# First batch in another order, FFN weight transposes spread over the tail, gate half of the in-projection in the third batch

## The chip, the cores and the metric

The kernel runs on one core of a Trainium2 chip. The metric is the device time of one execution in microseconds (us). The core has a matrix engine (PE, whose weight loads are listed as PEld), a vector engine (DVE), a scalar engine (ACT), GpSimd (POOL), and a queue engine (SP) that issues most DMAs. Every engine works through its own list of instructions in order, and the lists are tied together by semaphores alone.

## The reference

One layer over 64 sequences of 32 rows (D = 512), each with 257 context rows:

```python
x = x + cross_attention(layernorm(x), ctx, mask)        # 16 heads of 32
x = x + mamba(layernorm(x))
x = x + ffn_int8(layernorm(x))                          # 512 -> 2048 -> 512, quantised

# mamba: d_inner 1024, 16 states, 4 taps
x_, z = split(x @ in_proj_w)                            # z: the gate half
x_ = silu(conv4(x_) + conv_b)
B, C, d = split(x_ @ x_proj_w)
dt = softplus(d * dt_w + dt_b)
h_t = exp(dt*A) * h_(t-1) + dt*x_*B_t ;  y_t = sum_n h_t*C_t
y = (y + x_*D) * silu(z);  return y @ out_proj_w
# ffn: weights are quantised per row; the activations by their global maximum
```

## The kernel before

The 2048 rows are 16 tiles of 128 rows, and one tile is four sequences (batches b = 0 to 3). `schedule` is called once for each engine with a class that holds that engine's part of every step, so the text of `schedule` is the program order of every engine. It runs 17 stages: `interval(ta, tm, to, more)` does the attention of tile `ta`, the first part of the mamba of `tm = ta - 1` ("front"), and its end for `to = ta - 2` ("back"). Interval 0 has attention only (with the quantisation of the FFN weights), interval 1 has attention and front, intervals 2 to 14 have all three, interval 15 has all three but no next tile, and `tail` finishes the mamba of the last two tiles and starts the FFN phase.

Inside an interval each batch b does the following. PE computes `scores` (L987) for this batch, transposes the next batch's context (`kv_transpose`, L921), computes its keys (`kv_keys`, L955) and its values in two halves (`kv_values`, L966), transposes the probabilities (`transpose_p`, L996) and weighs the values (`weigh_values`, L1005). ACT copies each of these out of PSUM and takes the exponentials (`softmax`, L1245; `normalise`, L1282). DVE makes one pass over the scores of each head group (L1623) and the reciprocal of the sums (L1636).

The mamba work lies between these steps. The scan of a tile is 32 DVE steps in the order of `CHAIN`: for each of 8 channel chunks c a product (c,0) (L1736), a scan (c,1) (L1741, 4.4 us), a product (c,2) (L1747, 2.3 us) and a sum (c,3) (L1713, L1718). ACT makes the factors, `decays` (c, half), in 16 groups of eight exponentials (L1390). `place(name)` calls put them at named places of a batch, by the tables `FINISH`, `BEGIN`, `FINISH_DECAYS` and `BEGIN_DECAYS`.

In batch 0 of an interval stand `x1_write` (DVE, L1650; it waits for PE's `wo_product` of the interval before, L1020), `mamba_norm`, `mamba_turn` (PE, L1051), `mamba_in` (the x half of the in-projection, 64 matmuls, L1058), the taps on ACT (L1326), `mamba_conv` (DVE, L1677), the SiLU (ACT, L1333) and `mamba_bcd` (PE, L1085). In batch 1 stand `dt_row`, `mamba_steps`, `mamba_softplus` (ACT), `mamba_dt` (DVE, L1691), `mamba_gate` (the gate half, 64 matmuls, L1058), `mamba_gated`, `mamba_out` (PE, L1099), `gate_silu` (ACT, two table loads around two SiLUs, L1355 to L1357) and `out_sum` (DVE, L1821). `scores` of batch 2 waits for `out_sum`. In batches 2 and 3 come the next tile's queries (`ln_q_rows`, `q_transpose` L1027/L1240, `q_product` L1039, `q_spread` L1275); `kv_transpose` in batch 3 waits for the copy xnT (L1240), because both use bank 0. Batch 3 ends with `wo_product`.

`kv_keys` in batch b = 2 waits for `gate_silu`, because keys and in-projection share banks 6 and 7; for the same reason each half of `mamba_gate` waits for one `keys_copy` (L1224).

Of the kernel before, what the change touches and what calls it, by code (L numbers as in the profile page):

```python
# [6 lines left out]
P = 128  # L7
# [32 lines left out]
def perceiver_kernel(nc, x, ctx_kv, mask, Wq, bq, Wk, bk, Wv, bv, Wo, bo, Win, conv_w, conv_b, Wx,  # L40
# [13 lines left out]
    with ExitStack() as ctx:  # L54
# [216 lines left out]
        tail_summed = sem("tail_summed")  # L271
        tail_kept = sem("tail_kept")
# [16 lines left out]
        wq_loaded = [sem("w1q_loaded"), sem("w2q_loaded")]  # L289
# [40 lines left out]
        FINISH = {(0, "a"): range(21, 22), (0, "b"): range(22, 25), (0, "c"): range(25, 28),  # L330
# [7 lines left out]
        FINISH_DECAYS = {(0, "n"): ((6, 1),), (0, "t"): ((7, 0), (7, 1))}  # L338
# [9 lines left out]
        def tail(part):  # L348
# [4 lines left out]
            part.decays(PREV, ((6, 1), (7, 0)))  # L353
# [6 lines left out]
            part.decays(PREV, ((7, 1),))  # L360
# [5 lines left out]
            part.weigh(PREV, 6)  # L366
            part.mamba_conv(LAST)
            part.gate(PREV, 5)
            part.mamba_silu(LAST)
            part.mamba_bcd(LAST, 0)  # L370
# [24 lines left out]
            for c in range(1, IC):  # L395
# [3 lines left out]
                for n in range(6 * (c - 2), min(2 * FC, 6 * (c - 1)), 3) if c > 1 else ():  # L399
                    part.weights_transpose(range(n, min(2 * FC, n + 3)))  # L400
                if c == 2:
                    part.out_sum(PREV)
                    part.out_norm(PREV)
                    part.out_rstd(PREV)
                    part.out_rows(PREV)
                    part.out_max(PREV)
                part.gate(LAST, c - 1)
                part.weigh(LAST, c)
                part.sum_states(LAST, c)
# [19 lines left out]
        def schedule(part, engine):  # L429
            part.load_context(0)  # L430
            part.load_x(0)
            part.kv_transpose(0, 0)
# [4 lines left out]
            part.kv_values(0, 0)  # L437
            part.values_copy(0, 0)
            part.kv_values(0, 1)
# [10 lines left out]
            def interval(ta, tm, to, more):  # L450

                here, front, back = ta is not None, tm is not None, to is not None
                for b in range(BT):
# [14 lines left out]
                    if b == 0 and front:  # L468
                        part.x1_write(tm)
                        part.mamba_norm(tm)  # L470
                    if b == 0 and here:
                        part.load_bias(ta)
                        part.residual(ta)
                    if here:
                        part.scores(g, ta, b, to)
                    if following:
# [9 lines left out]
                    if b == 2 and here and more:  # L486
                        part.ln_q_rstd(ta + 1)
                    if b == 3 and back:
                        part.out_rstd(to)
                    if b > 0:  # L490
                        place("a")
                    if here:
# [12 lines left out]
                    if following:  # L505
                        part.kv_keys(g + 1, b, ta, tm, to, more)
                    if b == 0 and front:
                        part.mamba_rows(tm)
                        part.mamba_turn(tm, keys)
                    if following and b == 0:  # L510
                        part.kv_values(g + 1, 0)
                    if following and b > 0:
                        part.keys_copy(g + 1, 0)
                    if here:
                        part.normalise(g)
                    if b == 0 and front:
                        part.mamba_transpose(tm, keys)
                    if following and b == 0:
                        part.keys_copy(g + 1, 0)
                    place("n")  # L520
                    if following:
                        part.keys_copy(g + 1, 1)
                    place("k")
# [14 lines left out]
                    if b == 0 and front:  # L538
                        part.mamba_taps(tm, 0)
                        part.mamba_pad(tm, 1)  # L540
# [8 lines left out]
                    if following and b > 0:  # L549
                        part.kv_values(g + 1, 0)  # L550
# [22 lines left out]
                    if b == 1 and front:  # L573
                        part.gate_silu(tm)
                    if following:
                        part.kv_values(g + 1, 1)
                        part.values_copy(g + 1, 1)
                    if b == 2 and here and more:
                        part.q_transpose(ta + 1)
                    place("d")  # L580
                    if b == 0 and front:
                        part.mamba_bcd(tm, keys)
# [19 lines left out]
        class Part:  # L602
# [3 lines left out]
            def weights_prepare(self, b, name): pass  # L606
            def weights_load(self): pass
            def weights_transpose(self, pieces): pass
            def kv_transpose(self, g, rows): pass
            def kv_keys(self, g, b, ta, tm, to, more): pass  # L610
            def keys_copy(self, g, j): pass
            def kv_values(self, g, h): pass
# [77 lines left out]
        def wT_out(n):  # L690
            if n < FC:
                return w1qT[:, :, n * P:(n + 1) * P]
            j, q = (n - FC) // 4, (n - FC) % 4
# [30 lines left out]
        def _(sp):  # L724
# [3 lines left out]
            class Loads(Part):  # L728
# [87 lines left out]

                def weights_load(self):
# [3 lines left out]
                    for i in range(4):  # L821
                        sp.wait_ge(wq_stored[i], 16)
                    sp.dma_start(w1q, w1q_dram.rearrange("(i p) d -> p i d", p=P)).then_inc(wq_loaded[0], 16)
                    sp.dma_start(w2q, w2q_dram.rearrange("(j p) f -> p j f", p=P)).then_inc(wq_loaded[1], 16)
# [68 lines left out]
        def _(pe):  # L893
# [10 lines left out]
            class Products(Part):  # L904
# [4 lines left out]
                def kv_transpose(self, g, rows):  # L909

                    pe.wait_ge(ctx_loaded, 16 * (g + 1))
                    for i in range(2):
                        if i == 0:
                            wait(pe, v_copied, 2 * g - 1 if not isinstance(g, int) or g else 0)
                            wait(pe, xnT_copied, 1 if isinstance(g, int) and g == 1 else rows)
                        else:
                            wait(pe, v_copied, 2 * g)
                        for c in (2 * i, 2 * i + 1):
                            for h in range(2):
                                at = (c % 2) * KF + h * P  # L920
                                last = pe.transpose(bank[i][:, at:at + P], ctx_sb[:, h, c * P:(c + 1) * P], idf[:])  # L921
                        last.then_inc(ctxT_psum, 1)
# [9 lines left out]
                def kv_keys(self, g, b, ta, tm, to, more):  # L932
# [5 lines left out]
                    for j in range(2):  # L938
# [8 lines left out]
                        if b == 2 and tm is not None:  # L947
# [12 lines left out]
                def kv_values(self, g, h):  # L960
# [4 lines left out]
                    for c in range(DC):  # L965
                        last = pe.matmul(bank[h][:], ctxT[:, c, h * P:(h + 1) * P], wv_sb[:, c, :],  # L966
                                         start=(c == 0), stop=(c == DC - 1))
                    last.then_inc(v_psum, 1)
# [133 lines left out]
                def weights_transpose(self, pieces):  # L1102
                    for n in pieces:
# [7 lines left out]
                        for k in range(4):  # L1111
                            src = (w1q[:, n, k * P:(k + 1) * P] if n < FC
                                   else w2q[:, (n - FC) // 4, (4 * ((n - FC) % 4) + k) * P:(4 * ((n - FC) % 4) + k + 1) * P])
# [3 lines left out]
                def sum_states(self, t, c):  # L1117
                    i = item(t, c)

                    wait(pe, tail_gated, i - 1)  # L1120
                    for n in range(NS):
                        if n % (NS // 2) == 0:
                            pe.wait_ge(tail_weighed, 2 * i + 1 + n // (NS // 2))
                        pe.matmul(bank[i % 2][:, 0:P], idf[:], state(i)[:, n, :], start=(n == 0), stop=False)  # L1124
# [829 lines left out]
```

## Time and profile before

| what | us |
|---|---|
| median of 3 runs (2095.92 to 2097.03) | 2096.26 |
| the profiled execution's own time | 2097.7 |
| its span, first to last instruction | 2095.9 |
| an interval of the loop, from one end of `wo_product` to the next | 113.9 |
| busy in the interval 1033.96 to 1147.86: DVE / PE / ACT | 107.7 / 106.8 / 98.3 |
| from the end of interval 15 (1830.2) to the first FFN matmul (1971.8) | 141.6 |

Interval 1 lasts 107.8 us, interval 2 112.8 us, interval 15 113.4 us. PE's mean granted clock over the span is 0.971 of full speed. Busy time alone does not say which engine sets an interval: each engine waits a little at a few places, and what counts is which of those waits lies on the loop of releases that closes from one interval to the next.

### The profile page before, as it was taken

To read this page: it belongs to the slowest core of one execution; us is meant where nothing else is said; L and a number is where in the kernel's file an instruction comes from. 1 tells how busy PE (TensorE), PEld (TensorE's weight loads), DVE (VectorE), ACT (ScalarE), POOL (GpSimd) and SP (SyncE) were. 2 spreads that over 40 slices of the span, in tenths; PEclk is the share of its full clock that TensorE was granted. 3 is DMA by queue.
4 is the path that set the end of the run, shared out by engine and by line. 5 is a ranking of instruction groups with operands and counts; after the bars stand their busy time and mean duration, and the time that the engine had idled before them with its cause. 6 is when DMAs were issued, how large, how long until landed. Compare 5 with 4: busy or idle time off the path is not lost. (4 is left out here: it accounts for less than half of the span.)

```text
span 2095.9 us, 37583 instructions
## 1 busy us (share of the span) xinstructions
PE 1921.6 (92%) x11655; PEld 1360.5 (65%) x11670; DVE 1853.5 (88%) x2313; ACT 1675.9 (80%) x4617; POOL 475.2 (23%) x397
## 2 busy tenths in 40 slices
PE   7998999999999999999999999999999999667799
PEld 5676766667676666676666767666666667466444
DVE  1546999999999999999999899999999999998688
ACT  3358989888979889888889897988988888867484
POOL 1001213031413122131304131312213131300013
PEclk9999999999999999999999999999999999888899
DMA  9522333233342332333324334233333332230214
GB/s 280 211 81 86 76 92 82 83 83 88 72 110 65 75 99 61 101 81 88 76 80 87 94 70 98 71 76 94 71 101 81 88 75 77 61 122 11 71 40 141
DMA packets 93396, 188.55 MB, mean 90 GB/s; under 512 B 18768, under 2 KB 39904, under 8 KB 88160
## 3 DMA queue, kind: packets, MB, share of 16 engines
q1 hardware_dynamic: 78448, 133.32, 19.6%
q0 software_dynamic: 14832, 54.01, 13.9%
q8 instruction: 33, 0.54, 0.1%
q14 instruction: 83, 0.68, 0.1%
HBM read 116.12 MB, written 17.18 MB: 64 GB/s over the span
## 5 line engine op out<-in xcount | busy, mean ns | idle before, releaser
L1390 ACT ACTIVATE dA<-dt,A_sb 128x124 f32<-128x124 f32 x2048 | 616.1, 394 | 14.4 <-DVE dt L1691 10.2
L1741 DVE TENSOR_TENSOR_SCAN hb<-dA,hb 128x2048 f32<-128x2048 f32 x118 | 522.4, 4427 | 8.1 <-ACT dA L1390 4.3
L955 PE MATMUL bank<-ctxT,wk_sb 128*128 128x256 f32 x2048 | 463.7, 384 | 21.6 <-ACT ctxT L1208 15.3
L966 PE MATMUL bank<-wv_sb,ctxT 128*128 128x512 f32 x1024 | 463.2, 595 | 2.3 <-ACT ctxT L1208 2.3
L955 PEld LDWEIGHTS bank<-ctxT,wk_sb 128*128 128x128 f32 x2048 | 384.9, 191 | 86.4 <-ACT ctxT L1208 19.2
L1484 POOL DMA_DIRECT2D hb<-hb x103 | 93.3, 906 | 1023.6 <-DVE hb L1747 1009.1
L966 PEld LDWEIGHTS bank<-wv_sb,ctxT 128*128 128x128 f32 x1024 | 186.8, 191 | 195.9 <-issue 195.8
L1736 DVE TENSOR_TENSOR hb<-u,BC 128x2048 f32<-128x2048 f32 x118 | 270.4, 2291 | 5.7 <-DVE u L1703 2.6
L1747 DVE TENSOR_TENSOR hb<-hb,BC 128x2048 f32<-128x2048 f32 x117 | 268.0, 2290 | 1.1
L1058 PE MATMUL bank<-xn2T,win_sb 128*128 128x128 f32 x2048 | 236.4, 277 | 0.7 <-ACT xn2T L1307 0.7
L1058 PEld LDWEIGHTS bank<-xn2T,win_sb 128*128 128x128 f32 x2048 | 234.8, 194 | 1.9 <-ACT xn2T L1307 1.1
L1459 POOL TENSOR_SCALAR maskn<-maskb 128x257 f32<-128x257 f32 x64 | 146.5, 2290 | 182.8 <-DVE soft L1623 155.0
L1245 ACT ACTIVATE Pr<-Pr,soft 128x257 f32<-128x257 f32 x256 | 127.4, 507 | 62.2 <-DVE soft L1623 61.9
L1713 DVE TENSOR_TENSOR hb<-hb 128x512 f32<-128x512 f32 (+2 forms) x248 | 149.4, 602 | 4.5
L1677 DVE SCALAR_TENSOR_TENSOR xs<-xpad,convw,xs 128x128 f32<-128x128 f32 x384 | 106.8, 346 | 51.1 <-ACT xs L1326 49.4
L1208 ACT ACTIVATE ctxT<-bank,lastT 128x256 f32<-128x256 f32 x256 | 100.8, 476 | 58.7 <-PE bank L921 58.7
L1005 PEld LDWEIGHTS bank<-PT,V 128*128 128x128 f32 x1024 | 123.5, 194 | 28.6 <-issue 28.6
L1282 ACT ACTIVATE Pr<-Pr,soft 128x256 f32<-128x256 f32 x256 | 108.9, 503 | 27.5 <-DVE soft L1636 27.5
L1005 PE MATMUL bank<-PT,V 128*128 128x128 f32 x1024 | 127.6, 278 | 2.8 <-ACT PT L1299 2.8
L1224 ACT ACTIVATE KT<-bank,bqkv 128x256 f32<-128x256 f32 x256 | 106.0, 467 | 28.5 <-PE bank L955 28.5
L1231 ACT COPY V<-bank 128x512 f32<-128x512 f32 x128 | 74.8, 584 | 63.5 <-PE bank L1005 41.8
L1445 POOL TENSOR_SCALAR stats<-stats 128x1 f32<-128x1 f32 x48 | 53.2, 1108 | 289.2 <-DVE stats L1539 289.2
(158 smaller groups left out, 2606.8 us busy)
## 6 DMA issues: line engine op xcount, KB each, us to landing
hb<-hb POOLq DMA_DIRECT2D x103, 512.0 KB, 4.8
ctx_sb<-in_ctx_dram SPq DMA_DIRECT2D x64, 512.0 KB, 3.9
BC<-bcd_dram SPq DMA_DIRECT2D x32, 1024.0 KB, 7.1
maskb<-in_mask_Bx1x1xS_fk_dram SPq DMA_DIRECT2D x64, 128.5 KB, 3.3
wstage<-in_L_ffn_w_dram SPq DMA_DIRECT2D x4, 2048.0 KB, 11.9
x_sb<-in_x_dram SPq DMA_DIRECT2D x16, 256.0 KB, 3.5
win_sb<-in_L_attn_in_proj_w_dram SPq DMA_DIRECT2D x1, 4096.0 KB, 24.4
bo_sb<-bias_dram SPq DMA_DIRECT2D x64, 64.0 KB, 2.0
```

Of the source, the lines that this page charges most:

```text
L955: last = pe.matmul(bank[6 + j][:, (m % 2) * KF:(m % 2 + 1) * KF], wk_sb[:, c, m * P:(m + 1) * P], ctxT[:, c, :], start=(c == 0), stop=(c = ...
L966: last = pe.matmul(bank[h][:], ctxT[:, c, h * P:(h + 1) * P], wv_sb[:, c, :], start=(c == 0), stop=(c == DC - 1))
L1005: last = pe.matmul(bank[4][:, m * P:(m + 1) * P], V[:, h, m * P:(m + 1) * P], PT[:, h, m, :], start=(h == 0), stop=(h == 1))
L1058: last = pe.matmul(bank[6 + q % 2][:, e * P:(e + 1) * P], win_sb[:, c, n:n + P], xn2T[:, c, :], start=(c == 0), stop=(c == DC - 1))
L1245: act.activation(Pr[:, m, :], Pr[:, m, :], ACT.Exp, scale=-1.0, bias=soft[:, 0, m:m + 1], accum_out=soft[:, 1, m:m + 1]).then_inc(exp_done, 1)
L1282: act.mul(Pr[:, m, 0:KF], Pr[:, m, 0:KF], soft[:, 2, m:m + 1]).then_inc(p_ready, 1)
L1390: last = act.activation(dA[:, c % 2, n * BT:(n + 1) * BT, 1:], dt[:, c, :].rearrange("p (b s) -> p b s", s=S)[:, :, 1:], ACT.Exp, scale=A_ ...
L1459: pool.tensor_scalar(maskn[:], maskb[:], -NEG, 1.0, ALU.mult, ALU.mult).then_inc(mask_scaled, 1)
L1713: dve.tensor_tensor(tile[:, 0:n, :], tile[:, 0:n, :], tile[:, n:2 * n, :], ALU.add).then_inc(sum_step, 1)
L1736: ins = dve.tensor_tensor(tile, u[:, c, :].unsqueeze(1).broadcast_to([P, NS, P]), BC[:, 0:NS, :], ALU.mult)
L1741: ins = dve.tensor_tensor_scan(flat, dA[:, c % 2].rearrange("p n s -> p (n s)"), flat, 0.0, ALU.mult, ALU.add)
L1747: ins = dve.tensor_tensor(tile, tile, BC[:, NS:2 * NS, :], ALU.mult)
```

## The change

In batch 0 of an interval: `mamba_norm` follows `scores`; decays (6,1) stand ahead of the exponentials (a new place "s"), (7,0) at "n", (7,1) between the two halves of the taps ("h"); the first half of `kv_values(.., 0)` is ahead of `mamba_turn` and the second half after `mamba_in`; scan step 25 goes ahead of the convolution; `mamba_bcd` goes from the end of batch 0 to batch 1 behind `scores`; the table load behind the SiLU comes after the second values copy. `kv_transpose` on PE becomes `kv_turn` in two halves, and in batches 1 and 2 the first stands ahead of `scores`. `mamba_gate` goes from batch 1 to batch 2 (ahead of `transpose_p`), and `gate_silu` from batch 1 to batch 2 (ahead of the second values copy). In the tail the FFN weight transposes are spread (5, 3, then 4 for each chunk from the third on, w2 first, loaded earlier), `out_max` moves back behind `weigh`, and the last chunk's states are partly summed on DVE.

```diff
-        FINISH = {(0, "a"): range(21, 22), (0, "b"): range(22, 25), (0, "c"): range(25, 28),
+        FINISH = {(0, "a"): range(21, 22), (0, "b"): range(22, 26), (0, "c"): range(26, 28),
...
-        FINISH_DECAYS = {(0, "n"): ((6, 1),), (0, "t"): ((7, 0), (7, 1))}
+        FINISH_DECAYS = {(0, "s"): ((6, 1),), (0, "n"): ((7, 0),), (0, "h"): ((7, 1),)}
...
-                        part.mamba_norm(tm)
...
+                    if following and 0 < b < BT - 1:
+                        part.kv_turn(g + 1, 0, 0)
                     if here:
                         part.scores(g, ta, b, to)
+                    if b == 0 and front:
+                        part.mamba_norm(tm)
+                    if b == 1 and front:
+                        part.mamba_bcd(tm, keys - DC)
+                    if following and 0 < b < BT - 1:
+                        part.kv_turn(g + 1, 0, 1)
...
+                    if following and b == 0:
+                        part.kv_values(g + 1, 0, range(0, 2))
...
                     if b == 0 and front:
                         part.mamba_in(tm, keys)
+                    if following and b == 0:
+                        part.kv_values(g + 1, 0, range(2, DC))
...
                     if b == 1 and front:
                         part.mamba_softplus(tm)
+                        part.mamba_dt(tm)
+                    if b == 2 and front:
                         part.mamba_gate(tm, keys)
-                        part.mamba_dt(tm)
                     place("b")
...
-                    if b == 1 and front:
+                    if b == 2 and front:
                         part.gate_silu(tm)
                     if following:
-                        part.kv_values(g + 1, 1)
+                        part.kv_values(g + 1, 1, range(DC))
                         part.values_copy(g + 1, 1)
+                    if b == 0 and front:
+                        part.mamba_table(tm)
...
-                        if b == 2 and tm is not None:
+                        if b == 3 and tm is not None:
                             pe.wait_ge(zs_ready, 2 * tm + j + 1)
...
-                for n in range(6 * (c - 2), min(2 * FC, 6 * (c - 1)), 3) if c > 1 else ():
-                    part.weights_transpose(range(n, min(2 * FC, n + 3)))
+                if c > 1:
+                    part.weights_transpose(range(4 * c, 4 * (c + 1)))
...
+                    if t == LAST and c == IC - 1:
+                        dve.wait_ge(tail_weighed, 2 * i + 2)
+                        for k, n in enumerate((4, 2)):
+                            wait(dve, tail_folded, k)
+                            dve.tensor_tensor(state(i)[:, 8:8 + n, :], state(i)[:, 8:8 + n, :],
+                                              state(i)[:, 8 + n:8 + 2 * n, :], ALU.add).then_inc(tail_folded, 1)
```

## Rows read from the trace of the kernel before

**Rows 1.** Busy time by engine in two intervals; PEclk is the granted clock.

```profile
1033.96:1147.86 113.90, 106.77 (x673) 76.40 (x681) 107.70 (x135) 98.26 (x282) 30.87 (x24) 1.00 0.34 82
1261.21:1375.11 113.90, 108.26 (x673) 77.13 (x680) 107.73 (x134) 98.13 (x282) 29.48 (x24) 0.99 0.35 83
```

**Rows 2.** The same for batches 0, 1 and batches 2, 3 of one interval.

```profile
1033.96:1099.53 65.57, 61.02 (x390) 45.02 (x390) 60.07 (x89) 53.51 (x142) 7.37 (x10) 1.00 0.30 82
1099.53:1147.86 48.33, 45.75 (x283) 31.38 (x291) 47.63 (x47) 44.74 (x141) 23.50 (x15) 1.00 0.40 83
```

**Rows 3.** Timeline of DVE, that interval: start, us, instruction, idle before it.

```profile
1038.66 0.67 DVE L1650 TENSOR_TENSOR x<-bank,xbo 128x512 f32<-128x512 f32 x1
...
1043.34 0.18 DVE L1636 RECIPROCAL soft<-soft 128x4 f32<-128x4 f32 x1 [1.11 <-ACT Pr L1245]
...
1056.47 6.76 DVE L1677 SCALAR_TENSOR_TENSOR xs<-xpad,convw,xs 128x128 f32<-128x128 f32 x24 [2.44 <-ACT xs L1326]
...
1098.65 0.68 DVE L1821 CUSTOM_DVE_ANT_0 x<-bank,x 128x512 f32<-128x512 f32 x1
```

**Rows 4.** Timeline of PE, that interval.

```profile
1036.97 7.17 PE L955 MATMUL bank<-ctxT,wk_sb 128*128 128x256 f32 x32 [1.03 <-ACT ctxT L1208]
...
1064.45 1.93 PE L1085 MATMUL bank<-xs,wx_sb 128*33 128x128 f32 x16 [2.89 <-ACT xs L1333]
...
1075.41 7.31 PE L1058 MATMUL bank<-xn2T,win_sb 128*128 128x128 f32 x64
1082.55 1.04 PE L996 MATMUL bank<-idf,Pr 128*128 128x128 f32 x8
...
1086.86 1.95 PE L1005 MATMUL bank<-PT,V 128*128 128x128 f32 x16
...
1099.60 0.73 PE L987 MATMUL bank<-KT,Q 32*32 32x257 f32 x32 [0.49 <-DVE stats L1821]
...
1121.87 1.06 PE L921 MATMUL bank<-idf,ctx_sb 128*128 128x128 f32 x8 [0.79 <-ACT xnT L1240]
...
1130.73 3.72 PE L955 MATMUL bank<-ctxT,wk_sb 128*128 128x256 f32 x16 [0.77 <-ACT Q L1275]
```

**Rows 5.** Timeline of ACT, that interval.

```profile
1036.44 1.57 ACT L1208 ACTIVATE ctxT<-bank,lastT 128x256 f32<-128x256 f32 x4 [0.72 <-PE bank L921]
1041.23 0.51 ACT L1245 ACTIVATE Pr<-Pr,soft 128x257 f32<-128x257 f32 x1 [3.22 <-DVE soft L1623]
...
1082.30 2.42 ACT L1390 ACTIVATE dA<-dt,A_sb 128x124 f32<-128x124 f32 x8 [0.65 <-DVE dt L1691]
1084.62 0.56 ACT L1297 COPY PT<-bank 128x512 f32<-128x512 f32 x1
...
1095.78 1.28 ACT L1355 ACT_TABLE_LOAD   x1 [0.59 <-PE bank L1099]
...
1098.17 1.28 ACT L1357 ACT_TABLE_LOAD   x1
...
1112.63 0.82 ACT L1224 ACTIVATE KT<-bank,bqkv 128x256 f32<-128x256 f32 x2
...
1116.62 0.58 ACT L1231 COPY V<-bank 128x512 f32<-128x512 f32 x1
...
1121.13 0.59 ACT L1240 COPY xnT<-bank 128x512 f32<-128x512 f32 x1
```

**Rows 6.** Timeline of PE in the tail: equal groups of 32 matmuls.

```profile
1882.69 5.46 PE L1124 MATMUL bank<-hb,idf 128*128 128x128 f32 x32 [5.75 <-DVE hb L1785]
...
1904.92 6.25 PE L1124 MATMUL bank<-hb,idf 128*128 128x128 f32 x32 [3.48 <-DVE hb L1785]
...
1936.89 3.81 PE L1124 MATMUL bank<-hb,idf 128*128 128x128 f32 x32
```

**Rows 7.** Timeline of DVE in the tail.

```profile
1903.26 0.16 DVE L1830 TENSOR_TENSOR xmax<-xmax 128x1 f32<-128x1 f32 x1 [2.18 <-POOL xmax L1501]
...
1962.10 0.29 DVE L1801 TENSOR_TENSOR win_sb<-bank,win_sb 128x128 f32<-128x128 f32 x1 [6.00 <-PE bank L1126]
```

More of the change, by code:

```diff
@@ L352, in tail @@
             part.kept_sum(PREV)
-            part.decays(PREV, ((6, 1), (7, 0)))
+            part.decays(PREV, ((6, 1),))
+            part.weights_transpose(range(0, 5))
             part.mamba_rows(LAST)
@@ L359, in tail @@
             part.sum_states(PREV, 5)
[L360 removed]
+            part.decays(PREV, ((7, 0),))
             part.feed(PREV, 6)
@@ L366, in tail @@
             part.weigh(PREV, 6)
+            part.decays(PREV, ((7, 1),))
+            part.weights_transpose(range(5, 8))
             part.mamba_conv(LAST)
@@ L431, in schedule @@
             part.load_x(0)
+            part.kv_turn(0, 0, 0)
+            part.kv_turn(0, 0, 1)
             part.kv_transpose(0, 0)
@@ L436, in schedule @@
             part.group_keys()
-            part.kv_values(0, 0)
+            part.kv_values(0, 0, range(DC))
             part.values_copy(0, 0)
-            part.kv_values(0, 1)
+            part.kv_values(0, 1, range(DC))
             part.values_copy(0, 1)
@@ L487, in interval @@
                         part.ln_q_rstd(ta + 1)
+                    if b == 3 and here and not more:
+                        part.weights_first()
                     if b == 3 and back:
@@ L506, in interval @@
                         part.kv_keys(g + 1, b, ta, tm, to, more)
+                    if following:
+                        part.keys_copy(g + 1, 0)
+                    if following and b == 0:
+                        part.kv_values(g + 1, 0, range(0, 2))
+                    if here:
+                        part.normalise(g)
+                    if b > 0:
+                        place("n")
                     if b == 0 and front:
                         part.mamba_rows(tm)
[L509 to L520, printed above, removed]
                     if following:
                         part.keys_copy(g + 1, 1)
+                    if b == 0 and front:
+                        part.mamba_turn(tm, keys)
+                        part.mamba_transpose(tm, keys)
+                    if b == 0:
+                        place("n")
                     place("k")
@@ L539, in interval @@
                         part.mamba_taps(tm, 0)
+                    place("h")
+                    if b == 0 and front:
                         part.mamba_pad(tm, 1)
@@ L549, in interval @@
                     if following and b > 0:
-                        part.kv_values(g + 1, 0)
+                        part.kv_values(g + 1, 0, range(DC))
                     if following:
@@ L907, in top_spread, with kv_turn @@
                     spread(bank[0][:, 0:P], xmax[:, 0:1]).then_inc(top_psum, 1)
[L909 to L922, printed above, removed]
+                def kv_turn(self, g, rows, i):
+                    if i == 0:
+                        pe.wait_ge(ctx_loaded, 16 * (g + 1))
+                        wait(pe, v_copied, 2 * g - 1 if not isinstance(g, int) or g else 0)
+                        wait(pe, xnT_copied, 1 if isinstance(g, int) and g == 1 else rows)
+                    else:
+                        wait(pe, v_copied, 2 * g)
+                    for c in (2 * i, 2 * i + 1):
+                        for h in range(2):
+                            at = (c % 2) * KF + h * P
+                            last = pe.transpose(bank[i][:, at:at + P], ctx_sb[:, h, c * P:(c + 1) * P], idf[:])
+                    last.then_inc(ctxT_psum, 1)
                 def last_values(self):
```

65 lines of the change are left out of this document (44 added, 21 removed).

## The prediction

> **What bounds the kernel now.** I read the page's shares first, then the windows of single intervals, then the timelines of DVE, PE and ACT through one of them. The thirteen full intervals (2 to 14) are 1480 of the 2096 us, so they decide. In one, DVE is busy for 107.70 us of 113.90, PE for 106.77, ACT for 98.26 [rows 1]. In another PE is busy 1.5 us longer, at a mean granted clock of 0.99, and the interval lasts 113.90 us all the same [rows 1]: PE has slack and DVE sets the length. The reader is to see that DVE's idle time is mostly two waits: 1.11 us for the exponentials and 2.44 us for the taps of the convolution, both in batch 0 [rows 3]. PE's longest wait, 2.89 us for the SiLU ahead of `mamba_bcd` [rows 4], costs nothing now. The second thing to see is how full the halves are: in batches 2 and 3 (48.33 us) PE is busy 45.75, DVE 47.63, ACT 44.74; in batches 0 and 1 (65.57 us) it is 61.02, 60.07 and 53.51 [rows 2]. The change gives room in the half that has some and puts work into the half that has none.
>
> Times below count from the end of `wo_product` at 1033.96.
>
> **What it takes away.** Decays (6,1) go into ACT's idle 3.22 us ahead of the exponentials [rows 5]. ACT then runs through: context copies from 2.5 to 4.05, decays (8 take 2.3 net of overlap), exponentials 2.1, so the reciprocal starts at 8.4 instead of 9.4 [rows 3, 5]; `mamba_norm` now lies in DVE's wait of 1.11. Between the reciprocal (9.38) and its wait for the taps (22.51 less 2.44) DVE has 10.7 us of steps [rows 3], and now step 25 too, 2.3. The taps come ahead of that: with the half of `kv_values` behind it the in-projection starts 1.7 earlier, and only one group of decays stands before the first taps instead of three. So the convolution runs from 21.4 to 28.1 without its wait of 2.44; it ended at 29.3 with step 25 still to do [rows 3]. DVE is then 3.3 us ahead, and the first decays of tile `tm` (48.34 before [rows 5]) start at 45.0. `mamba_bcd` waits for less: `kv_turn` and `scores` (1.2) fill the front of its 2.89 and the table load behind the SiLU no longer holds back the values copy. If nothing else followed, 3.3 us an interval would be won.
>
> **What it moves.** The gate half is 64 matmuls, 7.14 from start to start [rows 4], and two SiLUs between two table loads, from 1095.78 to 1099.45, 3.67 [rows 5]. Both leave batch 1.
>
> In batch 1 they were cover. ACT copies the transposed probabilities only behind decays (0,0), at 50.66 [rows 5]; PE spent the time on the gate half and weighed the values at 52.9 [rows 4]. Now these copies come at 47.3 to 48.4, while PE has ended keys, transposes and values by about 44.5: a new wait of 4. That wait costs little by itself, because `scores` of batch 2 waits for `out_sum` on DVE anyway (its wait of 0.49 [rows 4]). It comes at 65.64 less 3.3, 62.3. PE gets there with 7.14 us owed.
>
> In batch 2 they meet a full ACT. I keep the old numbers here and take off the 3.3 at the end. The first half of the in-projection waits for the first `keys_copy` (0.8), the second for the second, which ACT ends at 79.5 (1112.63 and 0.82 [rows 5]; DVE's reciprocal and two groups of decays stand before it, none of them moved). So PE ends the gate half at 79.5 + 3.6 = 83.1. Transposes and values take 4.3 (1082.55 to 1086.86), weighing 1.95: 89.4 [rows 4]. Behind it ACT has, in order, a values copy, the oT copies, decays (3,1), then `gate_silu`, the other values copy and xnT. Without `gate_silu` that is 5.1 (1116.62 to 1121.72); with it 8.8 [rows 5], so xnT is there at 98.2. PE, with values (3.4), `q_transpose` (0.5) and `scores` (0.7) behind the weighing, is ready at 94.0 and waits 4.3 for xnT, where it waited 0.79. `kv_transpose` starts at 98.3 instead of 87.91 [rows 4]. From there to the end of `wo_product` it is 26.0 as before (1121.87 to 1147.86), less the 0.77 for the queries, whose copies no longer are late: 25.2 [rows 4].
>
> **The sum for an interval:** 45.0 (to the first decays) + 50.0 (98.3 less 48.34) + 25.2 = 120.2. The next interval's ACT work hangs on the same end (oT copies, 16 decays, values copy), so the loop closes through PE, ACT and DVE in turn, and DVE, then with 12 us idle, does not bound it. Against 113.9 that is +6.3.
>
> **PE's clock comes on top.** After a wait of 3.48 us 32 matmuls took 6.25 instead of 3.81, after 5.75 us 5.46: 1.65 to 2.4 lost to the granted clock at its lower level of the two, 1.2 instead of 2.4 GHz [rows 6]. The 2.89 us wait sometimes brings it as well, that is the interval with 108.26 busy [rows 1]. The wait of 4.3 in batch 3 lies on the loop; I take 1.7 for it, the lower row, because PE is denser here; bounds 0 and 2.4. The same loss in batch 1 is covered. So 121.9, +8.0 an interval, x 13 = +104.
>
> The Trainium skill's "ScalarE: Activation LUTs", section "What ACT_TABLE_LOAD costs", puts a switch of tables at 1.28 us for the load and about 1.38 us to drain, which would make `gate_silu` 6.4 and the interval nearly 125. The trace has no such drain: load, SiLUs and load fill 3.67 us end to end [rows 5], and I stay with that.
>
> **The rest.** Interval 1 gets the same new wait for xnT without DVE behind it: +5 (0 to +7). Interval 15 has no xnT; only `gate_silu` delays its batch 3, less the head start: +1.5 (-3 to +3). In the tail, DVE's wait of 2.18 for `out_max` goes; the last sum of 32 matmuls, behind which DVE waits 6.00 [rows 7], becomes 20 and two small additions, -2.7; fewer weight copies per chunk -1: together -6 (-10 to 0). The earlier load of w2 waits for keys of batch 2 that are done when SP comes to it. Setup and interval 0 do the same work in nearly the same order: 0. Sum +0.5.
>
> The profiled execution took 2097.7 (span 2095.9 and 1.8 around it), 1.4 above the median of the runs. 2097.7 + 104 + 0.5 - 1.4 = **2201 us**.
>
> **Rivals.** (a) *Faster: DVE stays the bound.* DVE loses its two waits, PE fits the gate half into batches 2 and 3, and ACT clears batch 2 in time. The interval is then DVE's 113.9 - 3.3 = 110.6, the total 2096 - 43 - 6 = 2047. For it speaks that DVE is the busiest engine [rows 1] and that DVE and PE alone would need only about 110: DVE from `x1_write` to `out_sum`, 57, and PE from there 52 to 53. It is what the Trainium skill's "Perfetto Trace Analysis", section "Identifying the Most-Contended Engine", would have one expect: improve the engine with the highest occupancy first. Against it: xnT would have to be ready 4.3 us earlier and the second `keys_copy` 1 us earlier, and nothing before them on ACT is moved. It decides from there: if xnT comes before `scores` of batch 3, this is the result. 11 in 100. (b) *The chain holds only in part,* for instance because ACT is ahead at the start of an interval or the clock stays up: 114.4 to 119 us an interval, 2103 to 2163. 13 in 100. (c) *The clock falls at both new waits and stays down longer,* or the decays of chunk 2 slip too: above 124, over 2228. 8 in 100. (d) *It cancels:* 113.7 to 114.1. 2 in 100. My forecast, 119 to 124 an interval, is 2163 to 2228: 66 in 100.
>
> **Chances and range.** Within 0.2% is about what a measurement of this kernel can tell from no change. Slower is forecast, (b) and (c): 0.87; same 0.02; faster 0.11. The range of 8 in 10 leaves out (a), (d), the upper part of (c) and the very lowest of (b): 2120 to 2232. The likeliest case has 2163 to 2228 by itself.
>
> **What would show it.** Intervals near 120 to 122 us. On DVE the two waits of batch 0 gone, and new waits in batch 3 (for PE's scores and for decays). On PE about 4 us idle ahead of `weigh_values` in batch 1, about 1 us inside the gate half in batch 2, about 4 us ahead of `kv_turn` in batch 3, ended by xnT, with the granted clock down behind it. `out_max` without a wait in the tail. The prediction is wrong if that last wait is under 1 us, or if the first decays of the tile don't start near 45.

## The result: 5.4% slower, and the profile after

| | before | after |
|---|---|---|
| median, us (lowest to highest) | 2096.65 (2095.92 to 2098.36), 4 runs | 2208.88 (2208.24 to 2210.72), 4 runs |
| span of the profiled execution, us | 2095.9 | 2208.9 |
| intervals 2 to 14 together, us | 1478.93 | 1588.70 |

The ratio of the medians is 1.0536, 95% interval 1.0517 to 1.0554. The forecast was 2201 (2120 to 2232).

The windows over intervals 2 to 14, first of before, then of after (busy time of PE, PEld, DVE, ACT and POOL; PEclk is the third number from the end):

```profile
237.88:1716.81 1478.93, 1399.06 (x8618) 999.80 (x8624) 1399.32 (x1729) 1275.90 (x3654) 384.98 (x312) 0.99 0.34 83
```

```profile
242.89:1831.59 1588.70, 1433.75 (x8618) 1040.76 (x8624) 1402.05 (x1730) 1284.53 (x3653) 371.43 (x312) 0.96 0.31 78
```

The matmuls are the same in number, DVE's busy time grew by 2.7 us, ACT's by 8.6. PE's grew by 34.7 at the same work, since its granted clock fell from 0.99 to 0.96. The rest of the 109.8 us, 75.1, is PE waiting. An interval is 122.21 on average, against 113.76.

The timeline of PE in the interval from 1098.61 to 1220.71 of after (start, us, instruction, idle before it and what ended it). Its lines have moved: `kv_turn` is L955, `weigh_values` L1040, the in-projection L1093, `q_product` L1074, `wo_product` L1055.

```profile
1111.92 0.63 PE L1086 MATMUL bank<-idf,ln_out 128*128 128x128 f32 x4 [1.90 <-ACT ln_out L1292]
...
1146.86 3.52 PE L1040 MATMUL bank<-PT,V 128*128 128x128 f32 x16 [3.70 <-ACT PT L1341]
...
1169.93 3.84 PE L1093 MATMUL bank<-xn2T,win_sb 128*128 128x128 f32 x32 [0.61 <-ACT KT L1266]
1174.57 3.84 PE L1093 MATMUL bank<-xn2T,win_sb 128*128 128x128 f32 x32 [0.79 <-ACT KT L1266]
...
1188.30 0.72 PE L1022 MATMUL bank<-KT,Q 32*32 32x257 f32 x32
1193.48 1.94 PE L955 MATMUL bank<-idf,ctx_sb 128*128 128x128 f32 x8 [4.46 <-ACT xnT L1282]
1195.21 4.96 PE L1074 MATMUL bank<-xnT,wq_sb 128*128 128x128 f32 x32
...
1217.01 3.70 PE L1055 MATMUL bank<-wo_sb,oT 128*128 128x512 f32 x8
```

The reader is to see one long wait in each half: 3.70 us for the transposed probabilities in batch 1, and 4.46 us for xnT in batch 3, where [rows 4] have 0.79. ACT in the same interval:

```profile
1143.34 2.42 ACT L1434 ACTIVATE dA<-dt,A_sb 128x124 f32<-128x124 f32 x8 [0.34 <-DVE dt L1735]
1145.66 0.56 ACT L1339 COPY PT<-bank 128x512 f32<-128x512 f32 x1
...
1173.68 0.83 ACT L1266 ACTIVATE KT<-bank,bqkv 128x256 f32<-128x256 f32 x2
...
1185.02 1.09 ACT L1333 COPY oT<-bank 32x128 f32<-32x128 f32 x4
1186.13 2.42 ACT L1434 ACTIVATE dA<-dt,A_sb 128x124 f32<-128x124 f32 x8
1188.57 1.28 ACT L1399 ACT_TABLE_LOAD   x1
1189.87 1.08 ACT L1399 ACTIVATE zs<-bank 128x512 f32<-128x512 f32 x2
1190.97 1.28 ACT L1401 ACT_TABLE_LOAD   x1
...
1192.74 0.59 ACT L1282 COPY xnT<-bank 128x512 f32<-128x512 f32 x1
```

From 1185.02 to xnT ACT runs without a pause: oT copies, eight decays, `gate_silu` with its two table loads, a values copy, xnT. PE was ready at 1189.0. And DVE, which has lost its wait for the taps (L1721, the row of [rows 3] with 2.44) but gained three waits in batch 3:

```profile
1106.45 0.18 DVE L1680 RECIPROCAL soft<-soft 128x4 f32<-128x4 f32 x1 [1.34 <-ACT Pr L1287]
...
1119.83 6.65 DVE L1721 SCALAR_TENSOR_TENSOR xs<-xpad,convw,xs 128x128 f32<-128x128 f32 x24
...
1189.31 0.43 DVE L1667 CUSTOM_DVE_ANT_0 Pr<-bank,maskn 128x257 f32<-128x257 f32 x1 [3.36 <-PE bank L1022]
...
1198.39 0.18 DVE L1680 RECIPROCAL soft<-soft 128x4 f32<-128x4 f32 x1 [3.18 <-ACT Pr L1287]
...
1208.57 4.42 DVE L1785 TENSOR_TENSOR_SCAN hb<-dA,hb 128x2048 f32<-128x2048 f32 x1 [4.07 <-ACT dA L1434]
```

The granted clock behind the two long waits, by windows of the same trace (PEclk is again the third number from the end):

```profile
1146.86:1150.27 3.41, 3.41 (x17) 3.41 (x18) 3.17 (x4) 2.17 (x8) 0.00 (x0) 0.54 0.00 0
1191.24:1198.06 6.82, 4.58 (x23) 4.61 (x24) 3.98 (x1) 5.42 (x14) 4.18 (x1) 0.52 0.16 55
```

It is the lower level, 1.2 GHz, for 3.4 us behind the first wait and for 6.8 us around the end of the second. In intervals 2 to 14 before had 8 such stretches, 27 us in all; after has 25, 123 us. Behind the first wait the stretch is 3.4 us long in 10 of the 13 intervals, at the second it is 6.8 us long in 10.

### The profile page after: what moved, and what is told of

The parts are those of the page before. It is cut to its first block, busy times and chain, and to the rows that moved or that the text cites. A ratio compares the mean times of both kernels' runs of the same rounds, so it can differ in the third digit from the quotient of the medians.

```text
span 2208.9 us, 37587 instructions
## 1 busy us (share of the span) xinstructions
PE 1959.2 (89%) x11658; PEld 1403.2 (64%) x11658; DVE 1855.5 (84%) x2315; ACT 1685.8 (76%) x4617; POOL 461.3 (21%) x397
## 4 chain that ended last, share of the span: by engine, by line
PE 41%; ACT 21%; issue 10%; DVE 9%; POOL 2%; SPq 1%; DMA 1%; DVEq 0%; ACTq 0%; POOLq 0%
ACT dA L1434 9%; PE bank L1000 8%; PE bank L1093 7%; PE bank L1134 4%; PE bank L1040 4%; PE bank L989 3%; PE bank L1074 3%; PE bank L1197 3%; PE bank L1219 3%; PE bank L955 2%; ACT Pr L1324 2%; POOL stats L1489 1%; ACT KT L1266 1%; DVE hb L1791 1%; PE bank L1031 1%
## 5 line engine op out<-in xcount | busy, mean ns | idle before, releaser
L989 PE MATMUL bank<-ctxT,wk_sb 128*128 128x256 f32 x2048 | 456.6, 381 | 3.5 <-ACT ctxT L1250 3.4
L1093 PE MATMUL bank<-xn2T,win_sb 128*128 128x128 f32 x2048 | 244.6, 280 | 18.9 <-ACT KT L1266 18.2
L1093 PEld LDWEIGHTS bank<-xn2T,win_sb 128*128 128x128 f32 x2048 | 236.6, 195 | 29.8 <-ACT KT L1266 26.0
L1503 POOL TENSOR_SCALAR maskn<-maskb 128x257 f32<-128x257 f32 x64 | 154.5, 2413 | 318.6 <-DVE soft L1667 317.3
L1040 PEld LDWEIGHTS bank<-PT,V 128*128 128x128 f32 x1024 | 138.2, 212 | 92.8 <-issue 92.8
L1040 PE MATMUL bank<-PT,V 128*128 128x128 f32 x1024 | 142.0, 298 | 57.4 <-ACT PT L1341 57.4
L955 PE MATMUL bank<-idf,ctx_sb 128*128 128x128 f32 x512 | 91.9, 317 | 77.2 <-ACT xnT L1282 62.8
L1667 DVE CUSTOM_DVE_ANT_0 Pr<-bank,maskn 128x257 f32<-128x257 f32 x256 | 94.2, 422 | 65.9 <-PE bank L1022 65.6
L955 PEld LDWEIGHTS bank<-idf,ctx_sb 128*128 128x128 f32 x512 | 67.7, 161 | 121.7 <-ACT V L1273 76.4
```

What stands on the lines that cost most here:

```text
L989: last = pe.matmul(bank[6 + j][:, (m % 2) * KF:(m % 2 + 1) * KF], wk_sb[:, c, m * P:(m + 1) * P], ctxT[:, c, :], start=(c == 0), stop=(c = ...
L1040: last = pe.matmul(bank[4][:, m * P:(m + 1) * P], V[:, h, m * P:(m + 1) * P], PT[:, h, m, :], start=(h == 0), stop=(h == 1))
L1093: last = pe.matmul(bank[6 + q % 2][:, e * P:(e + 1) * P], win_sb[:, c, n:n + P], xn2T[:, c, :], start=(c == 0), stop=(c == DC - 1))
L1503: pool.tensor_scalar(maskn[:], maskb[:], -NEG, 1.0, ALU.mult, ALU.mult).then_inc(mask_scaled, 1)
```

## The experiments

Lines with a minus are those of the kernel named first. Intervals given are means over 2 to 14.

**gate_back.** The changed kernel with the gate half and its SiLU back in batch 1; everything else of the change kept.

```diff
                     if b == 1 and front:
                         part.mamba_softplus(tm)
+                        part.mamba_gate(tm, keys)
                         part.mamba_dt(tm)
-                    if b == 2 and front:
-                        part.mamba_gate(tm, keys)
...
-                    if b == 2 and front:
+                    if b == 1 and front:
                         part.gate_silu(tm)
...
-                        if b == 3 and tm is not None:
+                        if b == 2 and tm is not None:
                             pe.wait_ge(zs_ready, 2 * tm + j + 1)
```

> The changed kernel with the gate half and its SiLU back in the second batch, all else as changed. Theory (the ACT chain of batches 2 and 3 makes the loss, the rest of the change gains): an interval of 110.6 to 112 us, no wait for xnT over 1 us, total 2050 to 2070, faster than before. Rival (the new order of batch 0 or the moved x projection is part of the loss): over 2097.

Measured: 2042.79 us (2040.98 to 2043.9), ratio to before 0.9749 (0.9733 to 0.9766). One interval by windows, and PE's scores of batch 3 and its wait for xnT in it:

```profile
1117.94:1227.98 110.04, 106.70 (x672) 76.43 (x679) 107.38 (x133) 98.39 (x282) 30.54 (x24) 1.00 0.36 88
```

```profile
1201.19 0.72 PE L1021 MATMUL bank<-KT,Q 32*32 32x257 f32 x32
1202.69 1.06 PE L954 MATMUL bank<-idf,ctx_sb 128*128 128x128 f32 x8 [0.79 <-ACT xnT L1281]
```

An interval is 110.22 us on average. In the one shown DVE is busy for 107.38 of 110.04 us and waits 0.39 us at most; its longest wait in all 13 is 0.86. So the new order of batch 0 by itself is a gain of 3.5 us an interval, and the whole loss lies in the moved gate half. Here DVE does bound the loop, as rival (a) had it: what failed that rival was the move, not its account of the engines.

Side by side with the interval of the changed kernel above (122.10), this one shows where the 12.1 us of the move lie. `scores` of batch 3 start 89.7 us into the interval there and 83.3 here: 6.4 us, the moved half on PE with the two waits inside it, less 1.3 us that PE is ahead when batch 2 begins. From these scores to `kv_turn` it is 5.2 there and 1.5 here: 3.7 us, the longer wait for xnT. From `kv_turn` to the end it is 27.2 there and 25.3 here: 1.9 us, where the clock is down. So about half of the loss is PE's own displaced work; the late copy and what follows from it are the other half.

**gate_only.** The opposite: the kernel before, with only the gate half, its SiLU and the wait for it moved.

```diff
                     if b == 1 and front:
                         part.mamba_softplus(tm)
-                        part.mamba_gate(tm, keys)
                         part.mamba_dt(tm)
+                    if b == 2 and front:
+                        part.mamba_gate(tm, keys)
...
-                    if b == 1 and front:
+                    if b == 2 and front:
                         part.gate_silu(tm)
...
-                        if b == 2 and tm is not None:
+                        if b == 3 and tm is not None:
                             pe.wait_ge(zs_ready, 2 * tm + j + 1)
```

> The kernel before with the gate half and its SiLU alone moved to the third batch. Theory: the whole loss and a little more, since the 3.3 us of the new batch 0 are missing: an interval of 123 to 126 us, total 2225 to 2260. Rival (the loss needs the other edits, such as the split context transposes): under 2200.

Measured: 2251.74 us (2251.37 to 2252.11), ratio 1.075 (1.0728 to 1.0771). An interval is 125.12, 11.4 more than before; in the new order the same move costs 12.0 (110.22 to 122.21). The timeline of PE:

```profile
1169.38 3.12 PE L1006 MATMUL bank<-PT,V 128*128 128x128 f32 x16 [3.84 <-ACT PT L1300]
...
1216.01 1.94 PE L922 MATMUL bank<-idf,ctx_sb 128*128 128x128 f32 x8 [4.47 <-ACT xnT L1241]
```

The two long waits come with the move alone. The prediction's sum without its gain of 3.3 is 48.34 + 50.0 + 25.2 + 1.7 = 125.2: the two parts add up nearly as separate terms.

**pt_first.** Is the wait of batch 1 part of the loss? The changed kernel with decays (0,0) behind the copies of the probabilities.

```diff
-        BEGIN_DECAYS = {(1, "b"): ((0, 0),), (1, "p"): ((0, 1),), (1, "c"): ((1, 0),), (1, "w"): ((1, 1),),
+        BEGIN_DECAYS = {(1, "p"): ((0, 0), (0, 1)), (1, "c"): ((1, 0),), (1, "w"): ((1, 1),),
```

> The changed kernel with decays (0,0) behind the copies of the transposed probabilities in the second batch, so that PE's new wait of 3.7 us there shrinks to about 1.4. Theory (that wait is covered by DVE and out_sum): within 4 us of the changed kernel's 2208.9. Rival (it is on the loop): 2.3 us less in each of 13 intervals, about 2179.

Measured: 2212.88 us (2211.14 to 2214.62), ratio 1.0564 (1.0543 to 1.0585); an interval 122.6. PE's timeline:

```profile
1142.33 2.02 PE L1040 MATMUL bank<-PT,V 128*128 128x128 f32 x16 [0.94 <-ACT PT L1341]
...
1147.28 7.13 PE L1134 MATMUL bank<-wout_sb,zs 128*128 128x512 f32 x16 [2.93 <-DVE zs L1864]
```

The wait is now in two pieces, 0.94 and 2.93, the second for DVE ahead of `mamba_out`. The time is not better: in batch 1 PE waits because it is ahead of DVE, and the wait is covered, whatever name it bears.

**no_tables.** Is it ACT's time ahead of xnT? The changed kernel without the two table loads of `gate_silu`; its two activations are Identity in place of SiLU, so the gate is not computed.

```diff
                         act.activation(tile[:, 4 * i:4 * (i + 1), :].rearrange("p e q -> p (e q)"), bank[6 + i][:],
-                                       ACT.Silu).then_inc(zs_ready, 1)
-                    act.preload_act_table_set("natural_log_exp_and_others")
+                                       ACT.Identity).then_inc(zs_ready, 1)
```

> The changed kernel with plain copies in place of the two gate SiLUs and their two table loads (the gate is not computed): 2.57 us less on ACT in the third batch, the same work on PE. Theory (ACT's chain to xnT sets the interval, and the granted clock falls because of the wait): PE's wait for xnT falls from 4.47 to 1.9, the clock stays up there, an interval of 117 to 119 us, total 2140 to 2165. Rival 1 (ACT sets it, the clock costs nothing): 119.8, total 2175. Rival 2 (the matmuls moved are the loss): over 2200.

Measured: 2144.03 us (2142.66 to 2145.39), ratio 1.0236 (1.0215 to 1.0256). ACT, then PE:

```profile
1271.22 1.08 ACT L1399 ACTIVATE zs<-bank 128x512 f32<-128x512 f32 x2
1272.65 0.62 ACT L1282 COPY xnT<-bank 128x512 f32<-128x512 f32 x1
```

```profile
1273.42 1.06 PE L955 MATMUL bank<-idf,ctx_sb 128*128 128x128 f32 x8 [1.76 <-ACT xnT L1282]
```

2.56 us less on ACT (two loads of 1.28) takes 2.70 off PE's wait and 4.4 off the interval (117.80). By the averages over intervals 2 to 14, `kv_turn` starts 2.4 us earlier, and from there to the end it is 25.4 instead of 27.4. The second part is the clock's: 12 lower stretches with 58 us are left, against 25 with 123, and none of them lies behind xnT. An interval is still 7.6 us longer than in gate_back, with the matmuls still in batch 2: that part is not the table loads. No run moved the matmuls without the two activations.

**silu_late.** Is it the order on ACT? The changed kernel with `gate_silu` one step later in batch 2, behind `q_transpose`, so that xnT is copied first. Nothing is taken away.

```diff
-                    if b == 2 and front:
-                        part.gate_silu(tm)
                     if following:
                         part.kv_values(g + 1, 1, range(DC))
                         part.values_copy(g + 1, 1)
...
                     if b == 2 and here and more:
                         part.q_transpose(ta + 1)
+                    if b == 2 and front:
+                        part.gate_silu(tm)
```

> The changed kernel with the gate SiLU behind the xnT copy instead of ahead of the second values copy; no work added or left out. Theory (the place of these 3.67 us in ACT's order is what PE waits for): the wait for xnT falls under 1 us, a smaller one of 1 to 2 us comes ahead of the queries' product or the second half of the keys, the clock stays up, an interval of 118 to 120 us, total 2150 to 2180. Rival (ACT is simply full in batches 2 and 3, the order does not matter): within 5 us of 2209.

Measured: 2164.21 us (2160.94 to 2169.02), ratio 1.0322 (1.0299 to 1.0346); an interval 119.25. ACT, then PE:

```profile
1284.05 0.59 ACT L1282 COPY xnT<-bank 128x512 f32<-128x512 f32 x1
1284.65 1.28 ACT L1399 ACT_TABLE_LOAD   x1
```

```profile
1284.78 1.07 PE L955 MATMUL bank<-idf,ctx_sb 128*128 128x128 f32 x8 [0.78 <-ACT xnT L1282]
1287.09 3.84 PE L1074 MATMUL bank<-xnT,wq_sb 128*128 128x128 f32 x32 [1.24 <-ACT zs L1399]
...
1295.33 3.69 PE L989 MATMUL bank<-ctxT,wk_sb 128*128 128x256 f32 x16 [0.95 <-ACT Q L1317]
```

PE's wait for xnT is back at its old size, but `q_product` now waits for the SiLU, and the keys for the queries. The clock did not stay up, as the theory had it: in 8 of the 13 intervals it falls for 3.4 us around the start of `q_product`. Order alone is worth 3.0 us an interval, the clock's part in it included, a third of the 8.5 by which the changed kernel's interval is longer than before. Against gate_back 9.0 us are left: by the averages `kv_turn` still starts 6.5 us later (91.2 instead of 84.7), although its wait is the same, and that is PE's moved half; the other 2.5 come behind it.

**filler.** What does the granted clock take? The changed kernel with 16 products that nothing reads (32 matmuls in the trace), put on PE in front of the scores of batch 3, that is into its wait for xnT.

```diff
+                def filler(self):
+                    for k in range(16):
+                        pe.matmul(bank[5][:, 0:P], idf[:], wo_sb[:, 0, 0:P], start=True, stop=True)
...
+                    if b == BT - 1 and following and front and back:
+                        part.filler()
                     if here:
                         part.scores(g, ta, b, to)
```

> The changed kernel with 16 matmuls of no use (3.6 us) on PE ahead of the fourth batch's scores in 13 intervals, inside PE's wait for xnT; only the clock can gain from them. Theory (after the wait PE runs at the lower clock and the loop pays 1.7 to 2.6 us): the granted clock stays up, an interval of 120 to 121 us, total 2175 to 2190. Rival (the clock is not on the loop): 2209 or more.

Measured: 2181.99 us (2179.78 to 2184.01), ratio 1.0415 (1.039 to 1.044). PE's timeline, and the windows of the wait in batch 1 and of the stretch from the filler on:

```profile
1290.45 3.74 PE L950 MATMUL bank<-wo_sb,idf 128*128 128x128 f32 x32
...
1295.72 1.07 PE L962 MATMUL bank<-idf,ctx_sb 128*128 128x128 f32 x8 [0.89 <-ACT xnT L1289]
```

```profile
1249.10:1252.52 3.42, 3.42 (x16) 3.42 (x17) 3.19 (x4) 2.17 (x8) 0.00 (x0) 0.51 0.00 0
1290.45:1300.20 9.75, 8.86 (x107) 8.28 (x105) 5.07 (x9) 8.79 (x22) 3.23 (x1) 1.00 0.17 55
```

xnT comes 0.1 us earlier on average, PE does 3.74 us of useless work, and the interval is 2.4 us shorter (119.83, just under what the theory gave). Nearly all of it lies behind `kv_turn`: 25.2 us from there to the end instead of 27.4. The clock stays at its upper level behind this wait and still falls behind the one of batch 1, where nothing was put. So the fall in batch 3 costs 2.2 to 2.4 us an interval. The one in batch 1 costs nothing that shows: `out_sum` starts at 61.0 us of the interval in the changed kernel, and at 60.9 in gate_back, which has no such fall.

**decays_back.** Which part of the new batch 0 gives the 3.5 us? gate_back with the decays at their old places.

```diff
-        FINISH_DECAYS = {(0, "s"): ((6, 1),), (0, "n"): ((7, 0),), (0, "h"): ((7, 1),)}
+        FINISH_DECAYS = {(0, "n"): ((6, 1),), (0, "t"): ((7, 0), (7, 1))}
```

> gate_back with the decays of chunks 6 and 7 at their places of before in batch 0 (all behind the exponentials; (7,0) and (7,1) together ahead of the taps), everything else of the new batch 0 kept. Theory (it is the place of these groups on ACT that takes away DVE's wait for the taps): the wait for the taps comes back with 1.5 to 3.5 us, intervals of 111.5 to 113.5 instead of 110.1, 2062 to 2090 us. Rival (the gain comes from kv_values in halves and the later mamba_bcd): intervals within 0.5 of 110.1, 2040 to 2050 us.

Measured: 2073.45 us (2067.49 to 2073.87), ratio 0.9884 (0.9869 to 0.9899), an interval 112.23. The time is what the theory gave, but DVE's wait is at another place. Its timeline:

```profile
1151.91 4.42 DVE L1784 TENSOR_TENSOR_SCAN hb<-dA,hb 128x2048 f32<-128x2048 f32 x1 [2.58 <-ACT dA L1433]
```

It is a scan that waits, where gate_back has no wait, for decays that ACT now makes too late; ahead of the convolution, further on, DVE has none. The places of the decays are worth 2.0 of the 3.5 us; the other 1.5 belongs to the rest of the reordering, which no run split further.

**old_tail.** What is the new tail worth? gate_back with the tail of before: its places of decays, weight copies and `out_max`, and its sums.

```diff
-                if c > 1:
-                    part.weights_transpose(range(4 * c, 4 * (c + 1)))
+                for n in range(6 * (c - 2), min(2 * FC, 6 * (c - 1)), 3) if c > 1 else ():
+                    part.weights_transpose(range(n, min(2 * FC, n + 3)))
...
-                    pe.matmul(bank[i % 2][:, 0:P], idf[:], xD[:, c, :], start=True, stop=False)
```

> gate_back with the tail of before (weight transposes 6 per chunk in pairs of three, decays grouped as before, out_max ahead of weigh, the last sum of 16 states with xD last); only w2 is still transposed first. Theory (the new tail is worth little: its two gains of about 3 us up to the first FFN matmul are eaten by the new order on ACT, by xD first, and by a lower granted clock in the FFN phase): 2041 to 2046 us, within 3 us of gate_back, first FFN matmul 3 us later counted from the end of interval 15. Rival (the tail edits are worth the 6 us of the prediction): 2048 to 2050.

Measured: 2044.43 us (2044.1 to 2047.23), ratio 0.9755 (0.9741 to 0.9768). The same time as gate_back: from the end of interval 14 to the end of the trace both take 373.6 us. Counted from there the first FFN matmul comes 1.2 us later, not 3 (counted from interval 15's own end, as the expectation had it, 0.7 earlier; interval 15 is 1.9 longer).

**xd_last** and **tail_mended.** Two tries to make the new tail pay, on top of gate_back: xD added last in every sum, as before; and with it decays (7,1) and three weight copies behind the SiLU.

```diff
-                    pe.matmul(bank[i % 2][:, 0:P], idf[:], xD[:, c, :], start=True, stop=False)
...
+                    pe.matmul(bank[i % 2][:, 0:P], idf[:], xD[:, c, :], start=False, stop=True).then_inc(tail_summed, 1)
```

```diff
-            part.decays(PREV, ((7, 1),))
-            part.weights_transpose(range(5, 8))
             part.mamba_conv(LAST)
             part.gate(PREV, 5)
             part.mamba_silu(LAST)
             part.mamba_table(LAST)
+            part.decays(PREV, ((7, 1),))
+            part.weights_transpose(range(5, 8))
```

> gate_back with xD added last again in every sum of states and nothing else. Theory (the wait for xD delays the first gate of the last tile by 3 us, and DVE passes it on): 1 to 3 us less than gate_back, 2040 to 2042. Rival (covered): the same time as gate_back within 1 us.

> gate_back with two edits in the tail: xD is added last again in every sum of states, and decays (7,1) with three weight copies stand behind the SiLU on ACT instead of ahead of it. Theory (PE's wait of 7.27 us for xD and the late SiLU cost the tail what the other edits won): PE no longer waits for xD, the first FFN matmul comes 2 to 5 us earlier than in gate_back, 2037 to 2041 us in all. Rival (DVE's scans set the tail, and PE's wait is covered): within 1 us of gate_back.

Measured: xd_last 2041.64 us (2040.66 to 2050.11), ratio 0.975 (0.9733 to 0.9767); tail_mended 2045.02 us (2041.48 to 2046.54), ratio 0.9756 (0.9742 to 0.9769). The first is what its theory gave, but only 1.15 us below gate_back, which the runs can't tell from its rival; the second lies outside both its theory and its rival. PE in gate_back and in xd_last, then DVE in tail_mended:

```profile
1836.34 0.77 PE L1157 MATMUL bank<-xD,idf 128*128 128x128 f32 x2 [7.89 <-ACT xD L1417]
```

```profile
1832.27 3.81 PE L1164 MATMUL bank<-hb,idf 128*128 128x128 f32 x32 [3.26 <-DVE hb L1827]
```

```profile
1811.70 4.42 DVE L1814 TENSOR_TENSOR_SCAN hb<-dA,hb 128x2048 f32<-128x2048 f32 x1 [2.52 <-ACT dA L1432]
```

PE's wait of 7.89 for xD is gone, but with the decays behind the SiLU the last scan of the tile before waits 2.52 for them. The four kernels with the whole new batch 0 and the gate half in batch 1 (gate_back, old_tail and these two) have ratios whose intervals overlap: their 2042 to 2045 us can't be told apart. Each is 2.4 to 2.5% faster than before.

## Why the prediction was right

**The bound and the loop.** The prediction read from [rows 2] that batches 2 and 3 had no room, and from [rows 4, 5] that xnT would be late. Both held. Taken apart at the same points, the interval from 1098.61 is 44.7 to the first decays (forecast 45.0), 50.1 from there to `kv_turn` (50.0) and 27.2 to the end (25.2, and 1.7 for the clock). By the averages over intervals 2 to 14 it is 44.7, 50.1 and 27.4; their sum of 122.21 stands against 121.9.

**What batch 0 gives.** Forecast 3.3, measured 3.5 (gate_back). The wait for the taps went, as forecast. That for the exponentials did not: it is 1.34 us in the changed kernel, though the reciprocal starts 7.8 us into the interval (forecast 8.4, before 9.4). It costs nothing there, as DVE has 10 us of idle time later; in gate_back it is mostly 0.7, and 0.39 in the interval shown.

**The waits.** Batch 1: forecast about 4 and covered, measured 3.70, and pt_first shows the cover. Inside the gate half: 0.8 and 1.0, measured 0.61 and 0.79. xnT: 4.3, measured 4.46. On DVE batch 3 has the forecast waits for scores and decays. The wait of 1.90 us for `ln_out` was not foreseen; gate_back has 1.79 at the same place in its interval of 110.04 us, so a wait of that size is harmless.

**The clock** was the term of the interval that was sized too low: 1.7 forecast, 2.2 by filler between `kv_turn` and the end (27.4 less 25.2; the forecast without the clock was 25.2 too) and 2.4 over the whole interval. That is near the upper of its two bounds from [rows 6]. The reason given for the lower one, that PE is denser here, did not hold: 10 of 13 waits of 4.46 brought 6.8 us at the lower level. The two intervals without any fall in batch 1 and with only 3.4 us of it in batch 3 (8 and 13) last 121.1 us; the others from the fourth on last 122.0 to 122.9. By pt_first, the cover in batch 1 did hold.

**Table loads.** The trace has no drain: the load starts 0.02 us behind the decays and takes 1.28, and the first activation starts 0.02 us behind its end. no_tables took away two loads and won 2.70 on PE's wait. The Trainium skill's "ScalarE: Activation LUTs", section "What ACT_TABLE_LOAD costs", adds about 1.38 us of drain to every switch, by which, as an estimate, some 2.8 us more would have gone; neither run nor trace bears it out.

**Rival (a)** fell by its own test: xnT came not before but 5.0 us after `scores` of batch 3 had begun. gate_back, where the gate half stays in batch 1, is what the engines do when ACT is in time: an interval of 110.22, where the rival had 110.6, and 2042.79 us, where it had 2047. The Trainium skill's "Perfetto Trace Analysis", section "Identifying the Most-Contended Engine", has one optimize the engine of highest occupancy first. This case shows both sides of it: the change took waits away from the busiest engine, DVE, and made the kernel slower, because PE's own moved work and the order on ACT (busy 98 of 114 us), which decides when PE goes on, then set the interval; with the gate half left in batch 1, the same relief of DVE is a gain.

**The outer terms.** The whole is 113.0 us by spans, where 104.5 was forecast:

| term | forecast | measured |
|---|---|---|
| intervals 2 to 14 | +104 | +109.8 |
| interval 0 | 0 | -1.3 |
| interval 1 | +5 | +6.35 |
| interval 15 | +1.5 | -1.35 |
| behind it | -6 | -0.4 |

Of the 5.8 missing in the first row, 1.8 is the base (an interval before is 113.76 on average, not 113.9); the other 4 are 0.3 an interval: the stretch behind `kv_turn`, where the clock is down, was 0.5 longer than forecast, the one before it 0.1, and the head start 0.3 larger. Outside the loop the errors of +1.35 and +5.6 stand against -1.3 and -2.85; that they leave only +2.8 is partly luck.

**The tail** was the step that was wrong in kind. Its pieces were there: the last sum is 20 matmuls, and the gate behind it waits 1.62 where [rows 7] have 6.00. But three things went against them. xD first makes PE wait for the last tile's xD and the gate behind that for PE; `out_max` still waits, 1.50 instead of 2.18; and the FFN matmuls ran slower. The tail of after, by the timelines of PE and of DVE:

```profile
2003.19 0.77 PE L1158 MATMUL bank<-xD,idf 128*128 128x128 f32 x2 [7.27 <-ACT xD L1418]
```

```profile
2008.95 0.29 DVE L1851 TENSOR_TENSOR win_sb<-bank,win_sb 128x128 f32<-128x128 f32 x1 [2.74 <-PE bank L1167]
...
2023.80 0.16 DVE L1880 TENSOR_TENSOR xmax<-xmax 128x1 f32<-128x1 f32 x1 [1.50 <-POOL xmax L1545]
...
2072.61 0.29 DVE L1851 TENSOR_TENSOR win_sb<-bank,win_sb 128x128 f32<-128x128 f32 x1 [1.62 <-PE bank L1167]
```

And the windows of the first FFN product, before, then after:

```profile
1971.80:2028.80 57.00, 56.26 (x248) 25.08 (x254) 48.16 (x81) 48.77 (x63) 0.00 (x0) 0.97 0.18 60
```

```profile
2082.18:2141.05 58.87, 58.52 (x256) 25.65 (x256) 49.09 (x81) 48.83 (x63) 0.00 (x0) 0.94 0.18 58
```

The first FFN matmul came 3.1 us earlier behind interval 15, and 2.7 were given back in the FFN phase, at a granted clock of 0.94 instead of 0.97. old_tail confirms the balance: old and new tail take the same time. Why the clock was lower there was not tested.

## What to carry to other kernels

Ahead of a move, look at how full each engine is in the part where the work goes, not over the whole loop, and at which small copies stand behind it in its engine's queue: here 7.1 us of PE and 3.7 us of ACT, moved from a half that covered them into a full one, cost 12 us an interval. About half of it was the moved PE work itself; the rest was a wait of 4.46 us for a copy of 0.6 that stood behind the moved ACT work, and the lower clock behind that wait. A wait counts only if nothing later on the loop waits longer anyway; two waits of about 4 us were worth nothing in one batch and all in the other. Split a change of several parts by undoing one: the half that was worth keeping (2.5% faster) was hidden under the half that cost 8%.

## What was not expected of the hardware

Useless matmuls in a wait made the kernel faster: 3.74 us more work on PE in each interval, 2.4 us less time, since the granted clock stayed at its upper level behind a wait that was cut from 4.46 to 0.89 us. By the rows here, waits of 3.70 us mostly brought 3.4 us at the lower level, waits of 4.46 mostly 6.8. The length of the wait alone does not fix it: in gate_only waits of 3.8 us brought 6.8 us in 9 of 13 intervals, in pt_first waits of 2.9 us in 5 of 13. In intervals 2 to 14 of gate_back, whose longest wait on PE is 2.44 us, it fell once.
